# Scores of a 16-head attention from two float32r parts, heads in two row halves, with maxima over 1024 keys and one V product for each quad

## The reference, cut to what matters

```python
def attn_b(x, qkv_w, qkv_b, out_w, out_b):          # B=2, S=1024, E=128, H=16 heads of 8
    qkv = (x @ qkv_w.T + qkv_b).reshape(B, S, H, 24)
    q, k, v = split(transpose(qkv, (2, 0, 3, 1)), 3, axis=2)
    scores = einsum('hbds,hbdt->hbst', q, k) / sqrt(8)
    w = softmax(scores, axis=-1)                    # over 1024 keys
    attn = einsum('hbst,hbdt->hbsd', w, v)
    return attn @ out_w.T + out_b
x = x + mix(layernorm(x)); x = x + ffn(layernorm(x))
x = x + attn_b(layernorm(x), ...)
x = x + ffn(layernorm(x))
```

## Time and profile before

| | |
|---|---|
| runs of the kernel before | 588.69, 589.48 and 590.08 us, median 589.48 |
| profiled execution, first to last instruction (span) | 586.6 us |
| between that span and the median of the runs | 2.9 us |
| mean granted TensorE clock over the span | 0.941 of 2.4 GHz |
| busy: PE, DVE, ACT, POOL | 536.7, 475.5, 343.4, 111.7 us |
| first maximum matmul, first exponential matmul | 155.72 and 183.47 us |
| last V product starts | 545.37 us |

### The profile page before, as it was taken

How to read it: one execution, slowest core, us unless ns; L and a number is a source line. 1 busy time by engine, 2 the same in 40 slices (tenths; PEclk the granted TensorE clock), 3 DMA queues, 4 the chain that set the end, 5 groups by cost and what they waited for, 6 DMA issues and landing times.

```text
span 586.6 us, 8035 instructions
## 1 busy us (share of the span) xinstructions
PE 536.7 (91%) x2831; PEld 228.8 (39%) x2831; DVE 475.5 (81%) x965; ACT 343.4 (59%) x667; POOL 111.7 (19%) x155
## 2 busy tenths in 40 slices
PE   2985899887399999999999999999999999999797
PEld 1442466564012333333333333333333333323376
DVE  6999667985499689898898988989889898843663
ACT  2765213244103577676776776767767677788441
POOL 6955914824200000000000000000000000010000
PEclk9996989997555799999999999999999999999999
DMA  8020000002340020200200200200200000000001
GB/s 200 26 55 18 1 1 1 6 26 86 122 121 22 1 84 5 78 2 1 82 2 1 82 2 1 82 3 2 81 2 1 1 2 2 1 2 1 1 20 54
DMA packets 14887, 18.77 MB, mean 32 GB/s; under 512 B 4040, under 2 KB 13175, under 8 KB 13687
## 3 DMA queue, kind: packets, MB, share of 16 engines
q1 hardware_dynamic: 14058, 17.54, 10.2%
q0 software_dynamic: 240, 0.46, 0.7%
q10 hardware_dynamic: 550, 0.27, 0.2%
HBM read 12.75 MB, written 4.19 MB: 29 GB/s over the span
## 4 chain that ended last, share of the span: by engine, by line
PE 73%; DVE 17%; DMA 3%; ACT 2%; issue 2%; SPq 1%; POOL 0%; ACTq 0%; DVEq 0%
PE ps L1255 20%; PE ps L1228 20%; PE ps L1293 19%; PE ps L1033 6%; PE ps L1043 5%; DVE acc L794 3%; DVE mx L895 3%; DVE h L710 2%; DMA k_scr<-gate 1%; DVE acc L840 1%; PE ps L1242 1%; DMA kt<-k_scr 1%; DVE st L687 1%; ACT acc L649 1%; DMA x<-in_L_attn_a_x 1%
## 5 line engine op out<-in xcount | busy, mean ns | idle before, releaser
L895 DVE TENSOR_REDUCE mx<-ps 128x1 f32<-128x512 f32 x512 | 314.4, 681 | 37.3 <-PE ps L1228 37.3
L649 ACT ACTIVATE gate<-ps 128x512 f32<-128x512 f32 x256 | 135.7, 629 | 81.5 <-PE ps L1293 81.5
L1228 PE MATMUL ps<-kt,qt 72*128 72x512 bf16 x384 | 157.8, 417 | 9.3 <-DMA kt<-k_scr 9.3
L649 ACT ACTIVATE acc<-ps 128x512 f32<-128x512 f32 x256 | 133.8, 629 | 48.5 <-PE ps L1293 48.5
L1293 PE MATMUL ps<-qt,kt 96*128 96x512 bf16 x384 | 145.2, 389 | 1.3 <-ACT gate L649 0.5
L1228 PEld LDWEIGHTS ps<-kt,qt 72*128 72x128 bf16 x384 | 38.4, 100 | 83.8 <-DVE mx L895 48.7
L1293 PEld LDWEIGHTS ps<-qt,kt 96*128 96x128 bf16 x384 | 37.4, 98 | 68.6 <-ACT gate L649 28.1
L1255 PE MATMUL ps<-gate,v 128*32 128x512 f32 x512 | 63.3, 613 | 0.0
L1255 PE MATMUL ps<-acc,v 128*32 128x512 f32 x512 | 61.8, 598 | 0.6 <-ACT acc L649 0.6
L447 POOL CAST nm_s<-nm 16x128 bf16<-16x128 f32 x16 | 4.6, 287 | 296.9 <-DVE nm L908 296.9
L1293 PE MATMUL ps<-val 96*128 96x512 bf16 x128 | 48.8, 381 | 0.0
(11 more groups left out here) (181 smaller groups left out, 474.9 us busy)
## 6 DMA issues: line engine op xcount, KB each, us to landing
qt<-q_scr SPq DMA_DIRECT2D x18, 192.0 KB
kt<-k_scr SPq DMA_DIRECT2D x18, 192.0 KB
val<-q_scr SPq DMA_DIRECT2D x6, 192.0 KB
val<-k_scr SPq DMA_DIRECT2D x6, 192.0 KB
x<-in_L_attn_a_x SPq DMA_DIRECT2D x4, 256.0 KB, 4.4
us<-h SPq DMA_DIRECT2D x8, 128.0 KB, 2.4
out<-x SPq DMA_DIRECT2D x4, 256.0 KB, 2.2
q_scr<-attn SPq DMA_DIRECT2D x6, 128.0 KB
```

The costliest lines, as they stand in the source:

```text
L649: act.activation(pexp[s % NPB][:, j, :], bank(exp_bank(n0, s * QH + j, last)[0]), ACT.Exp, scale=SCALE).then_inc(exp_done, 1)
L895: dve.tensor_reduce(mx[:, half, u // 2, u % 2:u % 2 + 1], bank(MBANKS[k % 4]), AX.X, ALU.max).then_inc(m_read, 1)
L1228: pe.matmul(bank(MBANKS[k % 4]), qt[r][0:QK_ROWS, half, j, c * P:(c + 1) * P], kt[r][0:QK_ROWS, keys, j, :], start=True, stop=True).then_i ...
```

## The change

- **Two float32r parts.** Part 0 of q and k is written by ScalarE as float32r (float32 storage, one matmul pass), part 1 is the remainder that VectorE writes at once. `second_parts`, GpSimd's third part and the buffer `qk_r` are gone. A head's rows are 2 x 2 x 8 = 32.
- **Two row halves.** The array's rows 0 to 63 hold one pair of the quad's heads (a = 0), rows 64 to 127 the other (a = 1); a matmul uses one half, with 62 rows for a maximum and 64 for an exponential (two shift rows instead of three). Between the two `max_mm` of a unit, which lie in one half, stand two exponential matmuls of the other half.
- **Maxima over 1024 keys.** PSUM is allocated in pairs of banks; a unit is both key halves of 128 queries in a pair, reduced by one VectorE instruction: 16 units for an item, two pairs of banks. `row_max` is gone. The negation moves to ScalarE (two small ACTIVATEs, the second as float32r); GpSimd has one subtraction left; the shift goes by four DMAs.
- **V at each step's end.** `pv(step - 1)` stands at the end of each step. The weights have 16 zero columns on either side, so that both halves of a quad accumulate in one bank; it is copied, turned and divided once for a quad. The copy stands on ScalarE behind the third exponential of the next quad's first step.
- **Layout.** The weights' columns and the biases are permuted at the start (a GpSimd copy, a small transpose, two more ScalarE copies), so that a store is 128 rows of 2 KB to contiguous DRAM. A chunk has 4 stores of 256 KB (before 6 of 128 KB), a quad 12 loads of 128 or 64 KB (before 6 of 192 KB).
- The last quad has no more banks than the others. The projections of chunks 0 and 1 stand in steps 2 and 3 of the last item.

```diff
-PARTS = 3
+PARTS = 2
+HALF = 64
-ORDER = "emememevm"
-E_MORE = 24
-MBANKS = (4, 5, 6, 7)
+MBANKS = ((4, 5), (6, 7))
-LEAD = 16
+LEAD = 8
+COPY_O_AFTER = 2
+HEADS = (2, 3, 0, 1)
...
@@ SyncE
-                for w, scr in ((0, q_scr), (1, k_scr)):
-                    sp.wait_ge(split_ready, 2 * c + w + 1)
+                for w, scr in ((0, q_scr[:, b, half, :, :, :]), (1, k_scr[:, b, :, :, half, :])):
+                    sp.wait_ge(wide_read, WIDE_QK + 2 * c + w + 1)
                     for i in range(PARTS):
-                        sp.dma_start(scr[i, :, c, :, :].rearrange("x j t -> j x t"),
+                        sp.dma_start(scr[i, :, :, :].rearrange("x j t -> (x j) t"),
                                      qk_s[c % 2][:, w, i, :]).then_inc(scr_done[c % 2], 16)
...
@@ ScalarE
+            def negate(hn):
+                act.wait_ge(e_mm, E_TURN_MAX[hn] + 1)
+                if hn:
+                    act.wait_ge(shift_in, hn * SHIFT)
+                src = bank(e_bank(E_TURN_MAX[hn]))[0:HT, 0:P]
+                act.activation(nm[:, :], src, ACT.Copy, scale=-1.0)
+                act.activation(nm_s[:, 0, :].bitcast(F32R), src, ACT.Copy, scale=-1.0).then_inc(e_read, 1)
+                act.wait_ge(e_read, E_TURN_MAX[hn] + 1)
+                act.sem_inc(nm_ready, 1)
...
@@ VectorE
+                dve.tensor_reduce(mx[:, item % 2, at:at + 1], pair(lo), AX.X, ALU.max).then_inc(m_read, 1)
...
@@ TensorE
+            def max_unit(u):
+                slot = M_UNIT[u]
...
+                if slot >= len(MBANKS):
+                    pe.wait_ge(m_read, slot - 1)
...
+            def e_free(slot):
+                if slot >= len(EBANKS):
+                    pe.wait_ge(e_read, slot - len(EBANKS) + 1)
...
+            for hn in range(NI):
+                n, half = divmod(hn, 2)
+                pe.wait_ge(shift_in, (hn + 1) * SHIFT)
+                for s in range(BT):
+                    step, u = hn * BT + s, HT * (hn + 1) + LEAD + 2 * s
+                    if u % HT == TURN_MAX_AT and hn + 1 < NI:
+                        turn_max(hn + 1)
+                    if s == TURN_O_AT and half == 0 and n:
+                        turn_o(n - 1)
+                    if hn == NI - 1 and s in PROJECT_AT:
+                        pe.wait_ge(m_read, M_UNIT[NU - 1] + 1)
+                        project(PROJECT_AT.index(s))
+                    for part in range(2):
+                        if u < NU:
+                            max_unit(u + part)
+                            max_mm(u + part, 0)
+                        exp_mm(hn, s, HEADS[2 * part])
+                        exp_mm(hn, s, HEADS[2 * part + 1])
+                        if u < NU:
+                            max_mm(u + part, 1)
+                    if step:
+                        pv(step - 1)
```

More of the change, by code:

```diff
@@ L15 @@
 F32 = mybir.dt.float32
[L16 removed]
+F32R = mybir.dt.float32r
 ALU = mybir.AluOpType
@@ L101, with e_bank, m_banks @@
 WIDE_F2 = WIDE_QK + 2 * NCH
-def exp_bank(n0, e, last):
-    if not last or e < E_MORE:
-        return EBANKS[(n0 + e) % 3], 3
-    ring = [EBANKS[(n0 + E_MORE + i) % 3] for i in range(3)] + [4, 5]
-    return ring[(e - E_MORE) % 5], 3 if e < E_MORE + 5 else 5
+def e_bank(slot):
+    return EBANKS[slot % len(EBANKS)]
+def m_banks(slot):
+    return MBANKS[slot % 2]
 def build(nc, ins, out):
@@ new lines, in e_free, with exp_mm @@
+            def e_free(slot):
+                if slot >= len(EBANKS):
+                    pe.wait_ge(e_read, slot - len(EBANKS) + 1)
+            def exp_mm(hn, s, j):
+                (n, half), slot = divmod(hn, 2), E_EXP[hn, s, j]
+                a, jj = divmod(j, 2)
+                rows, r = slice(a * HALF, (a + 1) * HALF), n % NBUF
+                e_free(slot)
+                pe.matmul(bank(e_bank(slot)), kt[r][rows, jj, s // TC, s % TC * P:(s % TC + 1) * P],
+                          qt[r][rows, half, jj, :], start=True, stop=True).then_inc(e_mm, 1)
@@ L1254, in pv, with loads @@
                 for j in range(QH):
[L1255 to L1256 removed]
+                    mm = pe.matmul(bank(O_BANK)[VW * j:VW * (j + 1), :], v4[n % NV][:, s, j, lo:lo + VW],
+                                   pexp[step % NPB][:, j, :], start=first, stop=last, tile_position=(0, VW * j))
                 mm.then_inc(pv_mm, 1)
[L1259 to L1261 removed]
+            def loads(n):
+                return (n // NBUF + 1) * LOADS + 32
```

496 lines of the change are left out of this document (207 added, 289 removed).

## The result

| | before | after |
|---|---|---|
| median of 6 runs each (lowest to highest) | 589.01 us (586.88 to 590.08) | **582.74 us** (581.16 to 585.01) |
| ratio, 95% interval | | 0.9899, 0.9875 to 0.9923 |
| span of the profiled execution | 586.6 us | 581.3 us (the run took 583.12) |
| first maximum matmul | 155.72 us | 146.41 us |
| first exponential matmul | 183.47 us | 176.94 us |

The change makes the kernel 6.3 us faster; 29.5 were forecast. The last row says where the rest is: the loop of 128 steps, which should have become 22 us shorter, takes as long as before. All of the gain is the earlier start.

What follows compares the result with a forecast made beforehand. TensorE was taken to bound the old loop. First exponential matmul at 175.5 plus 341 us of loop gave 516.5 against 546.4; a span of 557 plus 2.9 made 560.0 us, range 540 to 600.

Steps and rivals of the forecast that it cites:

- rival C: Loop: small waits pile up (array switches, late shift, starved VectorE), 0.2 to 0.3 us a step, 585 to 600; chance 0.08.
- a late start: Before the loop: if stores keep the old rate, the start costs 9 us; the range leaves room for it.
- D: Loop: ScalarE answers faster, so VectorE's 2.34 us bound the step, 15 less, 545; chance 0.77 together with the forecast.
- 128 steps: Loop: each step was to take 2.46 us, the longest of three candidate loops.
- all extras in the loop: Loop beside the steps: 7.5 maxima turns, 11.5 V's turn and copy, 1.9 projections, 4 low clock, 1.3 table load.
- the ring's size: Three exponential banks: fourth exponential matmul waits for the first's bank; 1.13 + 0.32 + 1.01 = 2.46 us a step.
- It doesn't depend on the slot: Step of 2.46 us: said to hold while three matmul slots stay under 1.13 us, up to 0.37 each.
- TensorE's old limit: Loop before the change: TensorE was said to bound it, 5.49 us between V blocks for two steps.
- rival A: Score matmuls: row halves don't run side by side, or float32r takes twice bf16; 2.90 us a step, 616 us; chance 0.09.
- The start: Before the loop: stores on 16 DMA engines, not 4; first maximum matmul at 147.8, not 155.7.
- the other end: Before the loop: stores at the old rate put the first maximum matmul at 156.8; cost 9 us.
- B: Loop: the clock falls because TensorE idles in every step; 3.7 us a step, about 720 us; chance 0.06.

Runs made afterwards that it cites:

- e2: Against the changed kernel, both score matmuls read the upper halves of the float32r words as bf16; 556.43 us, ratio 0.9458 to the kernel before.
- e12: Against the changed kernel, only the exponential matmuls read bf16 halves, maximum matmuls stay float32r; 579.01 us.
- e13: Against the changed kernel, every score matmul loads 64 of its 128 weight columns, moving side as before; 567.62 us.
- e1: Against the changed kernel, head order altered so exponential matmuls lie in the same row half as the maximum matmuls around them; 633.09 us.
- e5: Against the changed kernel, each store of q and k parts walks its 128 rows as 4 times 32; 595.71 us.
- e4: Against the changed kernel, exponentials and V are kept in bf16, so a V matmul is one pass; 530.91 us.
- e10: Against the changed kernel, score matmuls read bf16 halves, exponentials and V in bf16, copy of V moved to a quad's second step; 522.91 us.
- e11: Against the changed kernel, exponentials and V in bf16, and the copy of V behind the first exponential of a quad's second step; 534.39 us.
- e3: Against the changed kernel, the fourth exponential of each step and its matmul are left out; 538.52 us.
- e6: Against the changed kernel, the V products of two steps stand together at the end of every second step; 613.25 us.

## Why the prediction was wrong, point by point

The measured 582.74 us lies inside the range of 540 to 600, but only through the room left for rival C and a late start, and neither came in that form: that is luck. The forecast with D (542 to 580, 0.77) missed it.

| term | forecast us | measured us |
|---|---|---|
| first exponential matmul | 175.5 | 176.9 |
| 128 steps | 128 x 2.46 = 314.9 | 128 x 2.675 = 342.4 |
| all extras in the loop | 26.2 | 20.8 |
| from the last V product to the end | 40.6 | 41.2 |
| around the span | 2.9 | 1.8 |
| sum | 560.0 | 583.1 (the profiled run) |

- **The failed step is the ring's size.** Its mechanism was right: three banks, the fourth exponential matmul behind the first exponential, nothing passing it. But 1.13 and 0.32 us were read from matmuls of bf16 operands and carried over to float32r as they were. The measured 1.25 and 0.43 are 0.12 and 0.11 longer: the weight load of float32r takes twice as long and stands open at both places (e2, e12 behind the maxima, e13, e1). Of the 0.23, e2 gives back 0.20; most of the rest is that the first matmul in the earlier trace rows had its load partly hidden (in that trace the load begins 0.11 us ahead of it). With 0.01 less for the V block that is 0.215 us x 128 = 27.5 us, more than the whole miss of 22.7 us in the time.
- **"It doesn't depend on the slot"** was the sentence that hid this. It asked whether three slots fit into 1.13 us, and they do (0.34, then 0.24). It didn't ask whether the 1.13 itself was made of a matmul's own duration, which it is: 0.48 of it was the time from the matmul's start to the exponential.
- **TensorE's old limit** (2.745 us a step without extras) was removed, but the ring with float32r stands just below it, at 2.675, and the extras grew by as much as the steps shrank. By the forecast's own account of rival A the change would lose from 2.69 on.
- **The start** was right: stores on all engines, the loads then first, the first maximum matmul at 146.41 (147.8 forecast) and, by e5, the outermost count as the cause. The 9 us that I gave to the other end were too few: 13.3.
- **The extras**, 5.4 us too high in sum. The turn of the maxima costs 0.31 us (V blocks at 348.62 and 351.60, 2.98 apart), not 0.5; the copy and the turn of V 0.51 and 0.73 (steps of 3.19 and 3.41 us, in the chain of waits between V blocks at 225.63, 228.82 and 232.23), together 1.24 where 1.65 was forecast.

- **VectorE**: 1.135 us for a reduction of 1024 was right: back to back three take 3.47. It bounds e4 and e10 at 2.27 us a step.
- **The rivals.** A was told apart by e1: side by side they run, worth 50 us. B didn't come in the changed kernel: 1.00 from 200 to 504 us. C, small waits of 0.2 to 0.3 us a step giving 585 to 600, comes nearest in size but not in cause: not a switch, a late shift or a starved VectorE, but the load of weights. D didn't come either: VectorE stood idle 0.31 us in a step; its 2.27 us show only in e4, e10 and e11. None of my cases had a longer matmul in the ring at full rate.

## What to carry to other kernels

When a loop is bound by a ring (matmul, reader, bank free, matmul), its length is made of latencies of single instructions. A change of the operands' type changes these, even where the throughput stays: take each term of the ring and ask which type and shape its row had. Here a matmul right behind a wait paid its weight load in full, and one beside a slower matmul was answered no earlier than if it were slow itself. Read a step's length from several steps: in e3 long and short ones alternate, and in e6 a pair with a turn of the maxima takes 0.2 us more than one without. And before crediting a rewrite of a loop, split the measured gain by stage: here one line of a store's layout was worth 13 us in a change that brought 6.

## What the runs showed of the hardware

- A float32r score matmul has a weight load of 0.18 to 0.19 us for 128 columns and 0.13 for 64, where bf16 has 0.09 to 0.10 for 128. Behind a wait the matmul takes 0.50, 0.44 and 0.40 us in that order; with the load hidden 0.39.
- Two matmuls in different row halves start at most 0.01 us apart, in float32r as in bf16. A bf16 one beside a float32r one was answered as late as a float32r one (0.59 us, e12), and alone after 0.49.
- The clock after the maxima's end. With V in float32 TensorE kept 1.00 in the last items (500 to 510 us in the change, before). With V in bf16 it fell: e4 had 0.56 from 460 to 470 us. The level is then mostly 1.2 GHz. What went before was TensorE with only exponential matmuls and short V blocks to do. In e10 the fall was the same (0.52 to 0.62 from 450 to 490 us, 1.00 again from 490 to 500). That is rival B's event, in another kernel and another stage. In e4 a step without maxima took 2.00 us at the full clock (V blocks at 450.08 and 452.08) and 2.81 us at 0.50 (457.00, 459.81 and 462.62).
- Stores of 128 rows of 2 KB: 262 GB/s and 0.70 of the DMA engines with 128 as the outermost count, 102 GB/s and 0.26 with 4.
